# A selective-scan and expert kernel: states stay in PSUM over their decays, and PE sums the products with C in two banks

## The reference

```python
xz = rmsnorm(xn) @ in_proj_w.T ; x_s, z = xz[..., :256], xz[..., 256:]
u = silu(causal_conv4(x_s) + conv_b)
dt, B, C = split(u @ x_proj_w.T, [8, 16, 16])
delta = softplus(dt @ dt_proj_w.T + dt_proj_b)           # 256 channels
dA = exp(delta * A)  ; dBu = (delta * u) * B             # for each of 16 states
h[t] = dA[t] * h[t-1] + dBu[t]                           # scan over 512 positions
y[t] = sum over the 16 states of h[t] * C[t]
y = (y + u * D) * silu(z) ; return y @ out_proj_w.T + xn
# experts: top 2 of 8 for each of 4096 positions
out += gate_e * ((silu(xn @ w_gate[e]) * (xn @ w_up[e])) @ w_down[e])   # inner size 352
```

## Time and profile before

| what | value |
|---|---|
| median of 3 runs | 745.9 us (741.89 to 747.06) |
| the profiled execution's own time | 747.31 us |
| its span, first to last instruction | 745.5 us |
| mean granted TensorE clock | 0.881 of full speed |
| busy share DVE / PE / POOL / ACT | 91 / 75 / 75 / 57% |
| moved by DMA | 88.9 MB, mean 119 GB/s |

### The profile page before, as it was taken

How to read it: one execution, slowest core, us unless ns; L and a number is a source line. 1 busy time by engine, 2 the same in 40 slices (tenths; PEclk the granted TensorE clock), 3 DMA queues, 4 the chain that set the end, 5 groups by cost and what they waited for, 6 DMA issues and landing times.

```text
span 745.5 us, 12628 instructions
## 1 busy us (share of the span) xinstructions
PE 561.0 (75%) x3300; PEld 426.9 (57%) x3300; DVE 677.7 (91%) x1183; ACT 424.7 (57%) x780; POOL 560.7 (75%) x596
## 2 busy tenths in 40 slices
PE   2888775559887898869887899879885765566765
PEld 1357644347676676757676677667674433455544
DVE  6756879988999999998999899999999899999998
ACT  1688695216765566636765466736764355466660
POOL 4693089569789878987789778997678879975660
PEclk9958797769999899989999899989997869657888
DMA  6120020214655466653655456654642211212220
GB/s 206 45 58 1 0 96 19 65 40 125 197 177 198 139 197 186 203 164 117 197 179 198 135 174 203 204 162 140 181 162 98 75 55 51 82 28 71 55 70 18
DMA packets 54172, 88.89 MB, mean 119 GB/s; under 512 B 7760, under 2 KB 39008, under 8 KB 50896
## 3 DMA queue, kind: packets, MB, share of 16 engines
q1 hardware_dynamic: 48880, 78.25, 32.7%
q0 software_dynamic: 4496, 9.45, 5.0%
q10 hardware_dynamic: 720, 0.33, 0.2%
HBM read 78.86 MB, written 9.14 MB: 118 GB/s over the span
## 4 chain that ended last, share of the span: by engine, by line
DVE 36%; PE 31%; issue 13%; POOL 9%; ACT 8%; DVEq 2%; DMA 1%; POOLq 0%; ACTq 0%; SPq 0%
DVE h_sb L915 14%; DVE y_sb L932 12%; PE bank L1143 8%; PE bank L1160 7%; POOL dbu L710 5%; PE bank L1238 3%; PE bank L1232 3%; PE bank L1172 2%; DVE x_sb L970 2%; PE bank L1225 2%; ACT bank L424 2%; DVE ga L954 1%; PE bank L1205 1%; PE bank L1212 1%; POOL sp_m L349 1%
## 5 line engine op out<-in xcount | busy, mean ns | idle before, releaser
L710 POOL TENSOR_TENSOR dbu<-du,xn_all 128x512 f32<-128x512 f32 x196 | 247.3, 1283 | 39.9 <-DVE h_sb L915 35.0
L915 DVE TENSOR_TENSOR_SCAN h_sb<-bank,dbu 128x512 f32<-128x512 f32 x194 | 225.9, 1205 | 0.0
L1143 PE MATMUL bank<-id_sb,h_sb 128*128 128x128 f32 x1024 | 165.2, 306 | 66.8 <-DVE y_sb L932 61.8
L1143 PEld LDWEIGHTS bank<-id_sb,h_sb 128*128 128x128 f32 x1024 | 130.9, 156 | 116.1 <-issue 39.9
L932 DVE SCALAR_TENSOR_TENSOR y_sb<-bank,bc_sb,y_sb 128x256 f32<-128x256 f32 x480 | 196.0, 468 | 0.5 <-PE bank L1143 0.5
L424 ACT ACTIVATE bank<-delta,a_sb 128x512 f32<-128x512 f32 x194 | 132.6, 688 | 89.7 <-DVE h_sb L915 84.3
L501 ACT ACTIVATE xT<-bank 128x128 f32<-128x128 f32 x72 | 19.9, 276 | 126.7 <-PE bank L1219 126.2
L915 DVE TENSOR_TENSOR_SCAN h_sb<-da,bank 128x512 f32<-128x512 f32 x58 | 67.3, 1198 | 19.1 <-issue 8.3
L695 POOL DMA_INDIRECT xs<-xn_rows,src_now x72 | 72.6, 1009 | 11.5 <-issue 3.4
L1238 PE MATMUL bank<-xT,wgu_sb 128*118 128x128 f32 x432 | 64.8, 287 | 15.5 <-ACT ys L514 15.5
L1225 PE MATMUL bank<-wd_sb,hid 117*128 117x128 f32 (+1 forms) x432 | 65.1, 287 | 10.0 <-DVE hid L958 10.0
(11 more groups left out here) (174 smaller groups left out, 866.1 us busy)
## 6 DMA issues: line engine op xcount, KB each, us to landing
xn_all<-b_rows SPq DMA_DIRECT2D x25, 1024.0 KB
wgu_sb<-in_w_gu SPq DMA_DIRECT2D x72, 352.0 KB
wd_sb<-in_w_dn SPq DMA_DIRECT2D x72, 192.0 KB
y_slots<-ys SPq DMA_DIRECT2D x72, 64.0 KB
xn_rows<-xn_all SPq DMA_DIRECT2D x8, 256.0 KB, 2.3
out<-x_sb SPq DMA_DIRECT2D x7, 256.0 KB
x_sb<-in_x SPq DMA_DIRECT2D x2, 640.0 KB, 6.0
xs<-xn_rows,src_now POOLq DMA_INDIRECT x72, 3.3
```

The source lines that it names most:

```text
L710: nc.gpsimd.tensor_tensor(dbu[k % 2][:, hf, :], du[q][:, hf, :], b_ring[c % 2][:, k % CH, :], ALU.mult).then_inc(s["dbu_p"], 1)
L915: nc.vector.tensor_tensor_scan(h_sb[k % 2][:, hf, :], dec, inp, 0.0, ALU.mult, ALU.add).then_inc(s["h_rdy"], 1)
L1143: last = nc.tensor.transpose(HT[i][:, t % 2, hf * P:(hf + 1) * P], h_sb[k % 2][:, hf, t * P:(t + 1) * P], id_sb[:, :])
```

## The change

The state is scanned in place: DVE writes the scan over its own decay in the bank of `DAB`. C's row of each state is spread by DMA over all partitions, as B's was, into `c_ring` (the space of `xh_all`), so that C can be applied before the turn. DVE multiplies the bank by C's row into `h_sb` (`product`), and PE turns the product with the accumulate flag of a matmul, so that banks 2 and 3 hold the sum over the 16 states (`accumulate`). At the end ACT copies the two banks into `y_sb` (`y_evac`), and `y_turn` goes on as before. Batch 0 keeps the old way, except that its last sums go to the two banks. The banks of `DAB` are free only after the product (semaphore p_rdy), not after the scan; on ACT the second decay of a step moves behind th. B and C are no longer turned for batches 1 to 6.

```diff
@@ SP: rows of B and C
-                sp.dma_start(b_rows[bass.ds(b * S, S), :], bct_full[0:S, :]).then_inc(s["b_st"], 16)
+                sp.dma_start(b_rows[bass.ds(b * 2 * S, 2 * S), :], bct_full[0:2 * S, :]).then_inc(s["b_st"], 16)
...
+            def out_rows_in(b, c, first=False):
+
+                if first:
+                    sp.wait_ge(s["xh_pe"], NB)
+                else:
+                    wait(sp, "p_rdy", 2 * S * (b - 1) + 2 * CH * (c - 1))
+                sp.dma_start(c_ring[c % 2], b_rows[bass.ds(b * 2 * S + S + c * CH, CH), :].rearrange("(a s) t -> a (s t)", a=1).to_broadcast([P, CH * T])).then_inc(s[f"c_in{c % 2}"], 16)
...
                 for k in range(S):
+                    if k in (1, 4, 8):
+                        out_rows_in(b, 1 + k // 4)
+                    if k == 12:
+                        out_rows_in(b + 1, 0)
@@ ACT
             def decay_bank(b, q, k, hf):
 
                 m = 2 * k + hf
-                wait(act, "h_rdy", 2 * b * S + (m - 2 if m >= 3 else (-1, 0, 0)[m]))
+                if m >= 3:
+                    wait(act, "p_rdy", 2 * S * (b - 1) + m - 2)
+                elif isinstance(b, int) and b == 1:
+                    act.wait_ge(s["h_rdy"], 2 * S - 1 + m)
+                else:
+                    wait(act, "p_rdy", 2 * S * (b - 2) + (2 * S - 1, 2 * S, 2 * S - 2)[m])
...
                 if here:
                     slots_out(moe, k)
+                if not edge and k == 0:
+                    y_evac(b - 1)
                 if not edge:
                     decay_bank(*nxt, 0)
                 if prev:
                     out_out(moe, k)
+                if here:
+                    gate_out(moe, k)
                 if not edge:
                     decay_bank(*nxt, 1)
-                if here:
-                    gate_out(moe, k)
...
+            def y_evac(b):
+
+                act.wait_ge(s["y0"], TT)
+                for i in range(2):
+                    wait(act, "acc_mm", 2 * S * b - 1 + i)
+                    nc.scalar.activation(y_sb[:, 2 * i:2 * i + 2, :], HT[i], ACT.Copy).then_inc(s["y_out"], 1)
@@ DVE
-                    nc.vector.tensor_tensor_scan(h_sb[k % 2][:, hf, :], dec, inp, 0.0,
-                                                 ALU.mult, ALU.add).then_inc(s["h_rdy"], 1)
+                    nc.vector.tensor_tensor_scan(at, dec, inp, 0.0, ALU.mult, ALU.add).then_inc(s["h_rdy"], 1)
+
+            def product(b, k):
+
+                c = k // CH
+                if k % CH == 0:
+                    dve.wait_ge(s[f"c_in{c % 2}"], 16 * ((b - 1) * 2 + c // 2 + 1))
+                wait(dve, "acc_mm", 2 * (S * (b - 1) + k - 1))
+                for hf in range(NH):
+                    dve.wait_ge(s["h_rdy"], 2 * (b * S + k) + hf + 1)
+                    nc.vector.tensor_tensor(h_sb[k % 2][:, hf, :], DAB[(2 * k + hf) % 3][:, :], c_ring[c % 2][:, k % CH, :],
+                                            ALU.mult).then_inc(s["p_rdy"], 1)
...
-                if k > 0:
-                    sums(b, q, k - 1)
-                elif back:
-                    sums(b - 1, 1 - q, S - 1)
+                if back:
+                    product(b, k)
+                elif k > 0:
+                    sums(k - 1)
@@ PE
+            def accumulate(b, k):
+
+                wait(pe, "p_rdy", 2 * (S * (b - 1) + k + 1))
+                if k == 0:
+                    pe.wait_ge(s["g_sum"], 2 * b)
+                for i in range(2):
+                    for t in (2 * i, 2 * i + 1):
+                        for hf in range(NH):
+                            last = MM(HT[i][:, t % 2, hf * P:(hf + 1) * P], h_sb[k % 2][:, hf, t * P:(t + 1) * P], id_sb[:, :],
+                                      is_transpose=True, start=(k == 0 and t % 2 == 0 and hf == 0), stop=(k == S - 1),
+                                      skip_group_check=True)
+                    last.then_inc(s["acc_mm"], 1)
...
+                if back and k == S - 1:
+                    accumulate(b, k)
+                elif k == S - 1:
+                    h_turn(k)
```

More of the change, by code:

```diff
@@ L247, in fb, with turned @@
             return FB[hf] if isinstance(b, int) and b == 0 else FB[0]
+        def turned(b):
+            return isinstance(b, int) and b in (0, NB - 1)
         def in_bank(b, k):
@@ L334, in _ @@
             batch(NB - 2, None, True)
+            for c in range(1, S // CH):
+                out_rows_in(NB - 1, c)
             for b in range(NB - 1):
@@ L1178, in front @@
                     last.then_inc(s["br_mm"], 1)
-                if k == 10:
+                if k == 10 and turned(b):
                     pe.wait_ge(s["bct_rdy"], b + 1)
```

107 lines of the change are left out of this document (60 added, 47 removed).

## The result

The changed kernel takes **750.1 us** (median of 20 runs, 746.6 to 753.0), the kernel before 744.3 beside it (20 runs, 740.1 to 754.3). The ratio is 1.0084, 95% interval 1.0062 to 1.0105: slower by 0.8%, where 732 us was forecast. The two profiled executions have the same span, 745.4 and 745.5 us, but only because the part that the change does not touch ran shorter in the second: its first scan came at 45.26 us, and at 48.67 before, and steps 0 to 14 of batch 0 took 101.4 us for 104.2. Counted from the last step of batch 0, the first place that the change touches on DVE, the profile after is 6.1 us longer (598.8 against 592.7), which agrees with the medians.

The account below looks back on a forecast made before the run. DVE, PE and POOL nearly full in batches 1 to 5, DVE alone leading in 6 and 7. Terms 0, -8, -6 sum to -14: 747.3 to 733.3, median 1.4 lower, 732 us; 724 to 739 at 0.5, range 718 to 746.

Parts of the forecast that it names:

- Products 0.38 per step: On DVE, two products at 1.17 us replace four sums at 1.55 us per state, saving 0.38 us a step.
- scan output 0: DVE's scan writing its own bank costs 0, with bounds of -0.01 and +0.20 us per scan.
- the costlier product: Rival: products cost what the skip costs, 0.15 us more a step, 743 us; chance 0.2 together with small losses.
- the scan that pays for its bank: Rival: each scan pays +0.2 us for its bank output, +29 us, 761 us; chance 0.12 together with DMA.
- DMA: Rival: added megabytes make weights late, +20 to +40 us, 752 to 772 us; chance 0.12 together with the scan.
- Net 0: Batches 1 to 5: -0.3, +0.2, +0.6 (with the loop boundary), +0.1 and -0.3 us, taken as 0.
- th of step 8 0.9 us later: Middle batches, ACT: front work of step 7 begins 1.5 us later, and th of step 8 0.9 us later.
- From step 10 on six products save 2.3: Middle batches: DVE leads again from step 10, saving 2.3 us; step 11's Ln work gives back 0.9 to 1.1.
- The loop's boundary: PE's loop turn: last accumulation ahead of the branch may lose its cover, once, -0.9 to +2.1 us, taken as +0.6.
- Batch 6, -8: Batch 6: 6.1 us from products, a 2.29 us wait gone, y turned 0.6 earlier, 1.0 given back: -8 us.
- POOL is no reason for a loss: Middle batches' second half: POOL runs 35.2 us without pause, DVE's path becomes about as long; no loss from POOL.
- Batch 7, -6: Batch 7: 16 products save 0.38 us each, 6.1, with an end of the same length: -6 us.

Follow-up runs that it names:

- run 8: Changed kernel loading only every fourth of C's rows, so three of four products read stale rows: 749.9 us, ratio 1.007.
- run 4: Kernel before, with batch 6's first combination of gathered rows moved from step 2 to step 1: 747.0 us, ratio 0.998.
- run 7: Kernel before, with the loop over batches 1 to 4 written out on DVE and PE: 745.6 us, ratio 1.000.
- run 10: Kernel before, with ACT's softplus work of the next batch cut to 64 of 512 columns: 743.1 us, ratio 1.000.
- run 17: Kernel before, loops written out on DVE and PE, batch 6's first combination in step 1, its last two in batch 7: 740.7 us, ratio 0.997.
- run 3: Changed kernel with batch 6's first combination of gathered rows moved from step 2 to step 1: 744.5 us, ratio 1.0025.
- run 5: Changed kernel with the loop over batches 1 to 4 written out on DVE and PE: 745.9 us, ratio 1.0025.
- run 6: Changed kernel with the loop written out on DVE alone: 747.9 us, ratio 1.005.
- run 11: Changed kernel with batch 6's first combination in step 1 and the loop written out on DVE and PE: 738.9 us, ratio 0.9965.
- run 14: Run 11 with POOL's six softplus additions for batch 7, done in batch 6, on 64 of 512 columns: 737.5 us, ratio 0.993.
- run 15: Changed kernel with POOL's two gate multiplications in steps 2 and 3 of batch 6 on 64 of 512 columns: 744.1 us, ratio 1.002.
- run 18: Changed kernel with the loop and combination edits of run 17, ACT's order untouched: 740.2 us, ratio 0.997.
- run 9: Changed kernel with ACT's softplus work of the next batch cut to 64 of 512 columns: 739.9 us, ratio 0.993.
- run 12: Run 11 with ACT's second decay behind front work and tanh in steps 5, 8, 9 (batch 6: 9, 11, 12): 737.7 us, ratio 0.991.
- run 16: Run 13 plus late second decays in steps 8, 9 (batch 6: 9, 11, 12) and batch 6's last two combinations in batch 7: 727.6 us, ratio 0.979.
- run 13: Run 11 with ACT's second decay of steps 5 and 7 between the softplus's absolute value and its exponential: 741.9 us, ratio 0.994.

## Why the prediction was wrong

- **Products 0.38 per step, scan output 0: right.** 0.37 and 0 were measured, so the rivals that rested on them fell: the costlier product (743 us) and the scan that pays for its bank (761 us). The estimate of 0.66 us for a product from the Trainium skill's page "VectorE: DVE Perf Modes" (the section on the TRN2 errata) is not what this form takes between two starts: 0.59. Nor was it DMA (run 8).
- **The middle batches: the chain through ACT was right, its terms too small, and one was missing.** Net 0 was forecast for batches 1 to 5 with the end of batch 0 (the five terms as written add up to +0.3); it measured 8.4 (427.7 - 419.3) + 2.1 = +10.5. Batch 2, forecast +0.2, measured +3.8: step 0 +1.3, steps 1 to 8 +1.2, steps 9 to 14 -0.5, step 15 +1.8. The mean of step 0 over batches 2 to 5 rose by 0.5 (6.89 to 7.37), as forecast, but steps 0 to 3 together rose by 1.5 a batch, where about half a microsecond was forecast. That is no scatter of one execution: in batches 2, 4 and 5 they take 22.8 to 24.2 us in the five profiles with the old sums (before, runs 4, 7, 10, 17), mean 23.4, and 24.5 to 25.0 in the nine with the change and its order on ACT (changed kernel, runs 3, 5, 6, 8, 11, 14, 15, 18), mean 24.7. Where ACT has less to do (run 9) or its decays stand elsewhere (runs 12 and 16), some starts take 23.1 to 23.4 again. I had no term for PE's clock, which is low in step 0 or at the taps of step 2; why it costs the changed kernel more, no run shows. "th of step 8 0.9 us later" was too little: the step alone grew by 1.6. I had the second decay holding ACT's own work and missed that it holds PE too, through the absolute value and PE's in-order queue (runs 9 and 13). "From step 10 on six products save 2.3" counted two that don't: steps 10, 11, 13 and 14 saved 1.45, step 9 lost 0.3, step 12 0.6, which with its product is the 1.0 that I had given to Ln. Step 15 is the loop's.
- **The loop's boundary, +0.6 within -0.9 to +2.1: PE's branch I saw, DVE's I didn't.** A branch on either engine costs some 2.1 us when bare. DVE used to have four sums of the state before queued when it branched; now its last product waits for its last scan. Together 2.7 us in the profiles (run 5 against the changed kernel: step 15 of batch 2 -1.9, steps 0 and 1 of batch 3 -0.3 and -0.5), 4.4 by the ratios, whose intervals are as wide.
- **Batch 6, -8: the step that failed most.** It measured +0.5. In the sum I took DVE's busy time for DVE's own work. In the trace of before the five combinations of batch 6 take 3.58, 3.22, 1.12, 3.29 and 3.87 us, 15.1 in all, where 5 x 1.13 = 5.7 would do: 9.4 us of "busy" time was hold, and with DVE in another phase to POOL it became 21.5 - 5.7 = 15.8 (8.31, 3.99, 2.04, 3.83, 3.28). Runs 3 and 15 show the cause: the batch is 4.4 us shorter by moving one group, and the hold shrinks with POOL's run. The Trainium skill states the rule, and I did not weigh it: "SBUF — State Buffer", section "SBUF: two separate sides", says that DVE and GpSimd share a pair of ports under an exclusive lock, that a DVE operation with two SBUF inputs needs it against a GpSimd operation that reads SBUF, and that whoever starts first has it for the whole instruction. The trace agrees with the lock, but the hold outlasts one instruction: it lasted for six of POOL's. Products and sums have one tensor in a bank and were not held (products take 665 to 686 ns, the sums of 256 columns took 446 to 483); combinations have both in SBUF and were. The hold thus grew by 6.4 us. The tanh waits, 0.68 and 2.23, add 2.9: the later tanh of z stood behind Ln, Ln behind a decay, and the decay had waited 5.71 us for a product. Together 9.3, of which the forecast had allowed 1.0: that is the miss, within 0.2.
- **Batch 7, -6:** -4.9 measured (82.1 against 87.0): right in kind, 1.1 too much. **Batch 0's end, 0:** +2.1 in its last step, given back as -1.9 in step 0 of batch 1: right too.
- **"POOL is no reason for a loss": wrong**, not as a bound but because it holds DVE.
- The scan's output, by which I had priced a slower kernel, was not what made it slower; the terms for the middle, for batch 6 and for batch 7 were off by 10.5, 8.5 and 1.1 us. That is 20.1, and -14 + 20.1 = +6.1, the difference of the profiles.

Open: what decides in which step of a middle batch's start PE's clock is low, and with it about 1 us a batch of the loss (1.5 measured less 0.5 forecast); and what run 15 gained outside batch 6.
